# A fused audio-tower kernel: its prologue reordered, with products of zeros ahead of it and VectorE work handed to ScalarE and GpSimd

## The reference, cut to what matters

```python
dx = transpose(x[:, 1:] - x[:, :-1])          # v in the kernel, 8 channels
def step(levels, v):                          # one scan step, levels 1 to 4
    e = [v]
    for k in range(1, 4):
        e.append(_outer(e[-1], v) / (k + 1))
    for k in range(4):
        acc = levels[k] + e[k]
        for i in range(k):
            acc = acc + _outer(levels[i], e[k - 1 - i])
        new.append(acc)
...
h = sigs @ W.T + b
h = h + attention(layernorm(h))               # W / sigma for qkv and out
h = h + experts(layernorm(h))
```

## Time and profile before

| | us |
|---|---|
| median of 3 runs | 650.7 (650.46 to 653.05) |
| the profiled execution | 652.26 |
| its span in the trace | 650.3 |
| TensorE busy | 633.1 (97%) |
| VectorE busy | 405.8 (62%) |
| ScalarE busy | 304.1 (47%) |
| GpSimd busy | 321.2 (49%) |

### The profile page before, as it was taken

How to read it: one execution, slowest core, us unless ns; L and a number is a source line. 1 busy time by engine, 2 the same in 40 slices (tenths; PEclk the granted TensorE clock), 3 DMA queues, 4 the chain that set the end, 5 groups by cost and what they waited for, 6 DMA issues and landing times.

```text
span 650.3 us, 14315 instructions
## 1 busy us (share of the span) xinstructions
PE 633.1 (97%) x4237; PEld 531.2 (82%) x4239; DVE 405.8 (62%) x1033; ACT 304.1 (47%) x719; POOL 321.2 (49%) x336
## 2 busy tenths in 40 slices
PE   5979999999999999999999999999989999999998
PEld 3867888887888888788888778877769999999997
DVE  7876666666666665666666666777565455455540
ACT  3325444455454455444455544444573534443433
POOL 2355544455554455454445454444875315555551
PEclk9999999999999999999999999999999999999999
DMA  8521343343543343343343334111255623333232
GB/s 302 219 97 34 90 105 81 94 115 83 113 109 86 85 117 89 81 100 94 81 109 102 81 91 104 38 37 41 65 143 176 193 54 44 47 47 44 43 38 66
DMA packets 72262, 60.77 MB, mean 93 GB/s; under 512 B 6832, under 2 KB 60976, under 8 KB 71856
## 3 DMA queue, kind: packets, MB, share of 16 engines
q1 hardware_dynamic: 65600, 56.26, 31.9%
q0 software_dynamic: 6640, 4.22, 4.7%
HBM read 17.31 MB, written 26.82 MB: 68 GB/s over the span
## 4 chain that ended last, share of the span: by engine, by line
issue 32%; PE 31%; POOL 27%; DVE 6%; POOLq 2%; ACT 1%; DMA 0%; SPq 0%; ACTq 0%; DVEq 0%
PE bank L1292 29%; POOL z L497 6%; POOL e3l L492 5%; POOL g L486 4%; POOL e L479 4%; POOL z L499 3%; POOL rstd L506 3%; PE bank L1635 1%; DVE z L955 1%; POOL z L501 1%; POOLq L479 1%; PE bank L1471 0%; POOLq L505 0%; DVE ident_b L1128 0%; DMA h<-x_prev 0%
## 5 line engine op out<-in xcount | busy, mean ns | idle before, releaser
L1292 PE MATMUL bank<-whigh,uth 128*128 128x512 f32 x512 | 170.0, 412 | 1.2 <-DVE lowt L849 1.2
L1292 PEld LDWEIGHTS bank<-whigh,uth 128*128 128x128 f32 x512 | 89.6, 189 | 25.9 <-issue 7.4
L1292 PE MATMUL bank<-whigh,utl 128*128 128x512 f32 x256 | 101.2, 395 | 0.0
L585 POOL DMA_INDIRECT out<-prob,ids x39 | 60.9, 1561 | 66.8 <-ACT prob L803 66.8
L497 POOL TENSOR_TENSOR z<-z 128x512 f32<-128x512 f32 x32 | 42.6, 1332 | 100.4 <-DVE z L955 100.4
L506 POOL TENSOR_TENSOR rstd<-rstd,powers 128x1 f32<-128x1 f32 x64 | 35.2, 551 | 101.7 <-DVE rstd L942 55.0
L1292 PE MATMUL bank<-xvo,x 128*128 128x128 f32 x624 | 76.3, 275 | 0.0
L1292 PEld LDWEIGHTS bank<-xvo,x 128*128 128x128 f32 x624 | 72.8, 192 | 0.2 <-issue 0.2
L955 DVE TENSOR_TENSOR z<-bank,v 128x512 f32<-128x512 f32 x64 | 44.2, 691 | 31.6 <-PE bank L1292 27.8
L1292 PE MATMUL bank<-xT,qkw 128*128 128x128 f32 x512 | 62.5, 275 | 0.0
L1292 PEld LDWEIGHTS bank<-xT,qkw 128*128 128x128 f32 x512 | 59.8, 192 | 0.4 <-ACT xT L619 0.3
(11 more groups left out here) (231 smaller groups left out, 1351.8 us busy)
## 6 DMA issues: line engine op xcount, KB each, us to landing
sorted_rows<-blank SPq DMA_DIRECT2D x24, 709.5 KB, 5.5
xvp<-xvo SPq DMA_DIRECT2D x128, 128.0 KB, 2.3
w<-w_t SPq DMA_DIRECT2D x1, 4096.0 KB, 12.1
xvo<-sorted_rows SPq DMA_DIRECT2D x39, 64.5 KB, 1.8
out<-h SPq DMA_DIRECT2D x9, 256.0 KB, 3.3
w<-w_high SPq DMA_DIRECT2D x4, 512.0 KB, 6.4
x_columns<-x2t SPq DMA_DIRECT2D x32, 64.0 KB, 1.6
xg_in<-x_columns SPq DMA_DIRECT2D x8, 256.0 KB, 4.9
```

What stands on the lines that cost most here:

```text
L585: nc.gpsimd.indirect_dma_start(out=out[:, :], out_offset=bass.IndirectOffsetOnAxis(ap=ids[:, j:j + 1], axis=0), in_=y[:, 2 if j == SORTED ...
L1292: return T.matmul(out_, lhsT, rhs, start=start, stop=stop)
```

## The change

It has five parts. (1) `busy(12)` and `busy(9)`, products of zeros into a bank that is not in use, stand at the start of TensorE's list, around the first sum; VectorE clears `zeros` first. (2) `gram_qkv` moves ahead of tile 0's level 3; tile 0's products with uth for both halves come first, then those with utl; three later steps of tile 1 are exchanged. (3) The casts of `ident_b` and `mask` go from VectorE to ScalarE. (4) The sums of groups 1 to 3 are copied out of PSUM by ScalarE (`keep_sums`), into `e2`, and GpSimd adds them to `low` and `g3` (`add_sums`); the outer products of `low` for these groups go to GpSimd too. They stand behind GpSimd's iterations 0 and 1. (5) Steps of VectorE's prologue change their order (`signature_lo(0)` behind `features_lo(0)`, `level4(2)` behind the norm's steps).

```diff
@@ GpSimd
+            def outer_of_rest(out_, left, right):
+                shape = [P, TILES - 512 // C2, CHANNELS, CHANNELS]
+                return G.tensor_tensor(out_[:, rest, :].rearrange("p t (a c) -> p t a c", c=CHANNELS),
+                                       spread(left[:, rest, :], 3, shape), spread(right[:, rest, :], 2, shape), ALU.mult)
+            def add_sums(n):
+                pool.wait_ge(sums_kept, n)
+                for level in (low[:, groups[n], 1 + CHANNELS:LOW], g3[:, groups[n], :]):
+                    G.tensor_tensor(level, level, e2[:, groups[n], :], ALU.add).then_inc(rest_made, 1)
...
-            pool.wait_ge(small, SMALL_STEPS)
             add_channels(1)
+            iteration(0, True, True, True, False)
+            outer_of_rest(low[:, :, 1 + CHANNELS:LOW], t3, vh).then_inc(rest_made, 1)
+            pool.wait_ge(rest_made, 1)
+            pool.wait_ge(g3_outer, 1)
+            add_sums(1)
+            iteration(1, True, True, True)
+            add_sums(2)
+            add_sums(3)
+            pool.wait_ge(rest_made, 7)
             nc.gpsimd.iota(x2[:, :, DIM:ROW].bitcast(I32), pattern=[[P, TILES], [1, 1]], base=0,
-            iteration(0, True, True, True, False)
-            with pool.Fori(1, SCATTER_AT) as i:
+            with pool.Fori(2, SCATTER_AT) as i:
@@ ScalarE
             features_hi(0)
+            signature_hi(3)
             level3_hi(1)
-            signature_hi(3)
...
+            A.copy(ident_b[:], ident).then_inc(consts_cast, 1)
+            A.copy(mask[:], maskf).then_inc(consts_cast, 1)
...
+            keep_sums(1)
+            keep_sums(2)
             features_hi(1)
+            keep_sums(3)
@@ VectorE
             features_lo(0)
+            signature_lo(0)
...
-            V.tensor_copy(ident_b[:], ident).then_inc(consts_cast, 1)
-            V.tensor_copy(mask[:], maskf).then_inc(consts_cast, 1)
...
-            rest_made = low_outer(slice(per, TILES))
             features_lo(1)
-            first_norm(0)
-            first_norm_finish(0)
-            after(rest_made)
-            made = add_s2(1)
...
-            add_s2(2)
+            first_norm(0)
+            first_norm_finish(0)
@@ TensorE
+            def busy(n):
+                for _ in range(n):
+                    mm(B[0][:, 0:LEN], zeros[:, 0:P], zeros[:, 0:LEN])
+            pe.wait_ge(zeros_set, 1)
+            busy(12)
             pe.wait_ge(ld_before, 16)
             pe.wait_ge(small, 1)
             mm(B[1][:, 0:TILES * CHANNELS], before, v[:].rearrange("p t c -> p (t c)")).then_inc(s1_psum, 1)
...
+            busy(9)
             sum_level2(0)
             pe.wait_ge(ld_w, 16)
             weight_products(B[6:8], PAIRS, wqkv_sb[:, 0:PAIRS, :])
+            gram_qkv()
...
-            gram_qkv()
-            project_first_hi(0)
+            for half_ in range(2):
+                project_first_hi(half_)
+            for half_ in range(2):
+                project_first_mid(half_)
```

More of the change, by code:

```diff
@@ L133, in build @@
         e2 = e2.rearrange("p (t a) -> p t a", a=C2)
+        per = 512 // C2
+        groups = [slice(n * per, (n + 1) * per) for n in range(TILES // per)]
         xn_in, xp_in = (t.rearrange("p (t c) -> p t c", c=CHANNELS) for t in (xn_in, xp_in))
@@ L747, in _, with keep_sums @@
             low_features(1)
+            def keep_sums(n):
+                a.wait_ge(s2_psum, n + 1)
+                A.copy(e2[:, groups[n], :], B[SUM_BANKS[n]][:].rearrange("p (t c) -> p t c", c=C2)) \
+                    .then_inc(sums_kept, 1)
+            keep_sums(1)
+            keep_sums(2)
             features_hi(1)
+            keep_sums(3)
             level3_hi(2)
@@ L753, in _ @@
             a.wait_ge(norm_step, NORM_STEPS)
-            a.wait_ge(small, SMALL_STEPS)
+            a.wait_ge(consts_cast, 3)
             iteration(0, True, True, False)
@@ L857, in _ @@
             f2 = low[:, :, 1:1 + CHANNELS]
-            per = 512 // C2
-            groups = [slice(n * per, (n + 1) * per) for n in range(TILES // per)]
+            V.memset(zeros[:], 0.0).then_inc(zeros_set, 1)
             V.memset(low[:, :, 0:1], 1.0)
-            V.memset(zeros[:], 0.0)
             d.wait_ge(ld_x, 32)
@@ L871, in level2, with add_s2 @@
                 assert made == E2_STEPS[n]
[L873 to L883, removed]
+            def add_s2(then):
+                s2 = B[SUM_BANKS[0]][:].rearrange("p (t c) -> p t c", c=C2)
+                d.wait_ge(s2_psum, 1)
+                then(step(V.tensor_tensor(low[:, groups[0], 1 + CHANNELS:LOW],
+                                          low[:, groups[0], 1 + CHANNELS:LOW], s2, ALU.add)))
+                return step(V.tensor_tensor(g3[:, groups[0], :], g3[:, groups[0], :], s2, ALU.add))
             def by3(t):
@@ L915, in _ @@
             after(step(outer(g3[:, groups[0], :], t4[:, groups[0], :], v3[:, groups[0], :])))
-            made = add_s2(0, first_level3)
+            made = add_s2(first_level3)
             assert made == FIRST_GROUP_STEPS
@@ L1378, in project_first_hi, with project_first_mid @@
                     mm(B[1 + half_][:], uth[:, c, :], whigh[:, 0, c, col(half_, 512)], c == 0, False)
+            def project_first_mid(half_):
+                pe.wait_ge(u4_lo, 3)
+                for c in range(UC):
                     mm(B[1 + half_][:], utl[:, c, :], whigh[:, 0, c, col(half_, 512)], False, False)
@@ L1593, in _ @@
             accumulate(0)
[L1594 removed]
             pe.wait_ge(norm_step, OUT_COLUMN_STEP)
             mm(B[5][:, DIM + 1:DIM + 2], gram_out, wu_out[:]).then_inc(norm_mm, 1)
+            project(1, 1, UC + 1)
             x_columns(0)
[L1598 to L1600 removed]
+            project(1, UC + 1, 6)
+            pe.wait_ge(sums_kept, 1)
             pe.wait_ge(norm_step, SUMS_STEP)
             mm(B[6][:, 256:260], ones, nrm[:]).then_inc(norm_mm, 1)
[L1603 removed]
+            project(1, 6, 8)
+            sum_level3(2)
+            project(1, 8, 10)
             features(2)
[L1605 to L1606 removed]
+            pe.wait_ge(consts_cast, 3)
+            pe.wait_ge(sums_kept, 3)
             pe.wait_ge(norm_step, SQUARED_STEP)
```

29 lines of the change are left out of this document (7 added, 22 removed).

## The result

The changed kernel takes **662.15 us** (661.43 to 663.41, 4 runs), the kernel before 650.58 (649.23 to 653.05, 4 runs). The ratio is 1.0179, with a 95% interval of 1.0159 to 1.0200. So it is slower, as forecast, but by 11.6 us and not by 5.8, and outside the range. The profiled execution took 662.03, with a span of 660.2; that is 9.9 above the span of before.

What follows compares the result with a forecast made beforehand. TensorE was taken to bound the kernel, busy 97% of the span; -4.3 + 1.8 - 0.4 + 4.1 + 3.6 + 1.0 = +5.8 gave 658.1 profiled, 656.5 us on the median, range 648 to 660.5 (8 in 10).

Steps and rivals of the forecast that it cites:

- d: Prologue: net delay of VectorE's chain from the zeros ahead of the first sum, between -0.5 and +2.3, taken as 1.8.
- the cover: Prologue: busy(9), 2.0 us if the clock is up, lies beside VectorE's outer products; gone if the clock is slow.
- The rival with the slow clock at 10 us: Prologue: zeros don't bring the clock up, some 6 us more on the path, 662.5; chance 0.08.
- The -4.3: Prologue up to T0, the start of iteration 0: four gains of -0.9, -0.3, -1.5 and -1.6 together, before d.
- -0.9: Prologue: moving gram_qkv ends VectorE's wait of 1.64, but signature_lo(0) then waits some 0.8 for GpSimd; net gain 0.9.
- The other terms of the prologue: Before T0: mask cast -0.3 (tokbout takes over the 2.55 stall), GpSimd's z addition -1.5, TensorE's wait of 1.97 -1.6.
- The stalls: Iterations 1 and 2: GpSimd's inserted work delays root, xn and x2n, so TensorE waits; +4.1 and +3.6.
- The +1.0 for the clock: Iterations 1 and 2: TensorE's idle time of some 2.9 us in each lowers its clock; bounds nothing and 3.4.
- the 1.7 of a whole fall: Iterations 1 and 2: loss from one clock fall, three slow windows and parts of two; 1.2 us of it hidden.
- The rival in which each stall throws the clock back in full: Iterations 1 and 2: nothing hides the falls, which cost 3.4 in place of 1.0, 658.9; chance 0.18.
- the 1.28 of the earlier trace: Behind the loop: TensorE idle 1.28 before 484.77, then a window at 0.50 clock; sign that stalls lower the clock.
- iteration 0: Iteration 0: its small wait for tile 1's z additions goes, as these start relatively earlier; -0.4.

Runs made afterwards that it cites:

- e1: The changed kernel without the two filler calls busy(12) and busy(9); 655.07 us, ratio 1.0076 to the kernel before.
- e3: The changed kernel with both edits, e1's (no zeros) and e2's (GpSimd's block spread over gaps); 647.06 us, ratio 0.9948 to the kernel before.
- e2: The changed kernel, zeros kept, with GpSimd's outer products of low moved into iteration 0 and one addition into each of iterations 1 to 6; 653.17 us.
- e5: The changed kernel with the filler's tile set to 0.785 in place of 0; 661.69 us, ratio 1.0173 to the kernel before.
- e4: The kernel before with only busy(12) and busy(9) added and zeros cleared first; 658.26 us, ratio 1.0129.
- e8: e3 with gram_qkv put back behind tile 0's features; 647.06 us, ratio 0.9943 to the kernel before.
- e7: e3 with the outer products of g3 moved to iteration 0, those of low to 1, the additions to 2 to 7; 647.09 us.
- e6: The changed kernel with zeros filler 256 columns wide, 10 and 8 pairs in place of 24 and 18; 654.52 us, ratio 1.0072 to the kernel before.

## Why the prediction was wrong

- **The step that failed is d, the cost of the zeros**: +1.8 in the sum, some 5.3 in the trace of the changed kernel. By T0 less first sum the prologue without zeros is 3.1 to 3.4 shorter than before (e1, e3); with them T0 is 2.05 later, so they cost 5.2 to 5.4 there. The rows give the same: 2.31 at the first sum (6.26 against the 3.95 of the earlier trace rows), 2.15 at level 2's sum, and of the wait of 2.08 at tile 0's level 3 the 1.05 that e3 (1.03) doesn't have; 5.5 in all. In e2 and e5, where the pace rose sooner, this last wait is 0.78 and 0.90, and the zeros cost 3.9 to 4.2, as in e4 (4.15). I had bounded only the first of the three, by +2.3, about what came, and priced it at 1.8, near the slow level; for `busy(9)` I then took the cover as given "if the clock is up". The row at 14.99 of the earlier trace rows, 0.2 per pair after 11 us of mostly busy TensorE, spoke against that. The rival with the slow clock at 10 us got 0.08, and its mechanism is the one that happened. That its time of 662.5 was met as well is partly luck: its 6 us on top of the forecast are 3.5 in the trace, and other terms make up the rest.
- **In medians the zeros cost more**, 6.1 (e2 to e3), 7.1 (after to e1) and 8.0 (e4). The profiled executions of these pairs differ by 4.9, 6.2 and 5.1, of which 3.7, 3.6 and 4.2 are there at T3. The rest lies behind T3 and in how far a profiled execution is from its median, up to 2 us; no run shows its cause. The landing of the load explains little of it: with a first sum at 3.76, the earliest seen, the zeros would cost 0.2 more than with one at 3.95.
- **The -4.3 was 0.9 to 1.2 too large.** `gram_qkv` gives nothing where I put -0.9. VectorE's wait of 1.64 is gone and the lock of `signature_lo` is there as forecast (2.06). But it isn't the move of the products that takes this wait away: in e8, with them behind the features again, VectorE's x2n still follows with no wait, as the low part of the first weights, moved by part (5) of the change, now stands ahead of it:

```profile
18.45 2.14 DVE L881 TENSOR_TENSOR whigh<-w,whigh 128x1024 fp32r<-128x1024 f32 x1
...
20.62 0.29 DVE L1143 TENSOR_TENSOR x2n<-bank,uq 128x128 f32<-128x128 f32 x1
```

  And I left out that 24 products ahead of tile 0's level 3 delay it; VectorE waits in e3 1.03 for it, where before waited 0.17 and e8 not at all. By the traces the prologue is 4.1 shorter than before without the move (e8) and 3.4 with it (e3). Parts (3) and (5) were not run alone, so how the 4.1 divides among the other terms isn't shown. The row of e3:

```profile
14.13 0.69 DVE L925 TENSOR_TENSOR u<-bank,g 128x512 f32<-128x512 f32 x1 [1.03 <-PE bank L1308]
```

- **The other terms of the prologue came as forecast** in kind: in e3 the z addition takes 1.27 in place of 2.72, TensorE's wait of 1.97 for `wu_out` is gone, and `tokbout` takes over the stall with 2.62 in place of 2.55. The Trainium skill ("SBUF — State Buffer", "SBUF: two separate sides") has it that the shared ports are locked for the whole of an instruction; the trace agrees, as `tokbout` of e3 starts at 26.45 and ends 0.15 behind GpSimd's outer products of 2.84 from 26.08, and e7, with 0.28, shows that it is the meeting that costs and not the addition.
- **The stalls held**: +3.87 and +3.40 against +4.1 and +3.6, by the waits named. e2, with the same instructions spread over the gaps, has neither, so their cause is the place in the list.
- **The +1.0 for the clock was nothing in this trace, and right in size where the fall comes.** Idle times of 2.58 and 2.04 brought no fall in the profiled execution of the changed kernel. But e1, e5 and e6 have the same two stalls, and behind four of their six the granted clock falls to 0.50: in e1 in iteration 2, in e5 in both, in e6 in iteration 1. The rows of e5, TensorE in iteration 1 and windows of 1 us (busy, clock) in both:

```profile
71.08 0.33 PE L1424 MATMUL bank<-sq,xn 128*128 128x128 f32 x1 [2.59 <-DVE xn L1002]
75.83 0.27 PE L1433 MATMUL bank<-sq,x2n 128*128 128x128 f32 x1
...
73.00:74.00 1.00, 1.00 (x4) 0.50 0.00 0
...
90.00:91.00 1.00, 1.00 (x4) 0.50 0.00 0
```

  With the fall, iteration 1 takes 18.43 (e5) and 18.39 (e6) in place of 17.90, and iteration 2 takes 17.89 (e1, e5) in place of 17.43: 0.5 each, so 1.0 for two, the term as I had it. The mechanism is the one forecast too: the wait for x2n (0.83 and 0.91 above) is gone at 75.83, so of the 1.7 of a whole fall 0.5 is left. The rival in which each stall throws the clock back in full is out by its size. The rule of the Trainium skill ("TensorE: Matmul & The Clock Gate", "HAM oscillation") that I had weighed, of bursts of matmuls that start throttled behind each wait, agrees with four of these eight stalls and not with the other four; its example has waits longer than its bursts, so it was not just this case. The fall behind the 1.28 of the earlier trace rows comes no more surely: all fourteen profiles have a wait of 1.28 to 1.30 there, and only before, e4, e7 and e8 have the fall. What decides this isn't settled.

Put together: 5.8 + 3.5 (d) + 1.0 (the -4.3) - 1.0 (clock) - 0.4 (stalls 0.2 each too large) - 0.2 (iteration 0) = 8.7, the 8.75 measured at T3. To the 11.6 between the medians some 2.8 are missing: 1.1 lie behind T3, and the profiled execution of before lies 1.7 above its median, that of after 0.1 below.

## What to carry to other kernels

Filler ahead of real work on an in-order engine is only free where it ends before that work's data lands, at the slow level's price; read from the trace whether it changes the pace at all before costing what stands behind it. Work handed to an engine with idle time has to stand in its list directly ahead of a wait, and be no longer than this wait: the same instructions cost 7 to 9 us behind the z additions and nothing that these runs can show a few lines further down. A step moved out of a wait has to be priced at its new place too, as the qkv products were not, and the wait may go by another part of the same change. A stall's effect on the clock has to be read from more than one profile: one without a fall doesn't show that there is none.

## What the hardware showed that I had not expected

- Forty-two pairs of load and product of 64 columns, back to back for 9.9 us (1.09 to 10.95), with only the first sum among them, left TensorE at 1.2 GHz, whether of zeros or of 0.785; with pairs of 256 columns, equally back to back, the pace doubled near 5.5 us. In both the granted clock reads 1.00 throughout, so at the start of a program that column says nothing of the pace; the durations do.
- With the same program up to there, the clock falls near 20 us in some profiles (0.50 in e2 and e5 from 21 to 24) and not in the changed kernel's, whose 40 qkv pairs took 5.75 where e2's took 4.46. What decides this isn't settled.
